# Context rows of a decoder block turned on the host instead of on TensorE

## What is computed

```python
q = query @ Wq + bq
kvp = kv @ Wkv + bkv            # kv: the context, (8, 750, 512)
k, v = jnp.split(kvp, 2, axis=-1)
...
scores = jnp.einsum('bhqd,bhkd->bhqk', q, k) * scale + bias[None]
attn = jax.nn.softmax(scores, axis=-1)
```

## Time and profile before

| | |
|---|---|
| median of 3 runs | 1767.23 us (1766.71 to 1767.92) |
| span of the profiled execution | 1770.0 us |
| TensorE matmul busy | 1686.0 us (95%) |
| TensorE weight load busy | 1356.3 us (77%) |
| VectorE busy | 1073.6 us (61%) |
| ScalarE busy | 746.3 us (42%) |
| GpSimd busy | 750.8 us (42%) |
| middle phase | about 164 to 697 us |

### The profile page before, as it was taken

How to read it: one execution, slowest core, us unless ns; L and a number is a source line. 1 busy time by engine, 2 the same in 40 slices (tenths; PEclk the granted TensorE clock), 3 DMA queues, 4 the chain that set the end, 5 groups by cost and what they waited for, 6 DMA issues and landing times. The chain is left out here.

```text
span 1770.0 us, 34943 instructions
## 1 busy us (share of the span) xinstructions
PE 1686.0 (95%) x11125; PEld 1356.3 (77%) x11125; DVE 1073.6 (61%) x1895; ACT 746.3 (42%) x1345; POOL 750.8 (42%) x852
## 2 busy tenths in 40 slices
PE   7999999999999998898998999899999999999998
PEld 6787778887887777676777677678888888888876
DVE  5554465555565555777888888764664546446653
ACT  3224333343344425665556464522442424224441
POOL 3100332323333325878878657541542424215441
PEclk9999999999999999999999999999999999999999
DMA  7736766666665857999787676345564737346773
GB/s 217 243 138 174 213 184 176 185 174 176 171 190 167 217 143 148 186 204 173 169 183 161 144 155 169 92 136 184 179 233 107 243 97 245 101 140 206 239 247 89
DMA packets 211842, 309.53 MB, mean 175 GB/s; under 512 B 21856, under 2 KB 151600, under 8 KB 207232
## 3 DMA queue, kind: packets, MB, share of 16 engines
q1 hardware_dynamic: 191584, 232.40, 50.0%
q0 software_dynamic: 15392, 41.02, 10.6%
q10 hardware_dynamic: 4752, 34.61, 5.2%
HBM read 224.30 MB, written 83.66 MB: 174 GB/s over the span
## 5 line engine op out<-in xcount | busy, mean ns | idle before, releaser
L2193 DVE TENSOR_REDUCE part_max<-a_s_bank 112x1 f32<-112x500 f32 (+1 forms) x368 | 224.3, 670 | 58.6 <-PE a_s_bank L1913 44.8
L2088 ACT ACTIVATE a_prob<-a_st_bank 125x448 f32<-125x448 f32 x384 | 196.4, 545 | 110.7 <-PE a_st_bank L1936 93.9
L2899 DVE TENSOR_TENSOR e_u_sb<-e_u_bank,e_b_row 128x512 f32<-128x512 f32 x134 | 92.3, 689 | 229.8 <-PE e_u_bank L2656 215.0
L2654 PE MATMUL e_u_bank<-e_w_hi,e_xT_hi 128*128 128x512 f32 x536 | 214.3, 400 | 0.9 <-DVE e_w_lo L2892 0.4
L2655 PE MATMUL e_u_bank<-e_w_lo,e_xT_hi 128*128 128x512 f32 x536 | 209.9, 392 | 0.0
L2656 PE MATMUL e_u_bank<-e_w_hi,e_xT_lo 128*128 128x512 f32 x536 | 209.5, 391 | 0.0
L2715 ACT ACTIVATE e_g_hi<-e_g_bank 128x256 fp32r<-128x256 f32 x133 | 51.0, 384 | 343.1 <-PE e_g_bank L2663 341.1
L2816 POOL DMA_INDIRECT out<-l_rows,e_y_row x33 | 52.9, 1604 | 290.0 <-DVE l_rows L2942 163.3
L1763 POOL TENSOR_TENSOR a_part_sum<-a_prob 125x448 f32<-125x448 f32 x128 | 148.4, 1164 | 25.3 <-ACT a_prob L2088 25.0
L997 POOL TENSOR_TENSOR m_prob_sum<-m_prob 112x224 f32<-112x224 f32 x128 | 85.3, 670 | 157.7 <-ACT m_prob L1249 150.6
L2792 POOL TENSOR_TENSOR e_w_lo<-e_w_raw,e_w_hi 128x1024 fp32r<-128x1024 f32 x28 | 102.7, 3678 | 48.9 <-ACT e_w_hi L2725 48.9
(11 more groups left out here) (428 smaller groups left out, 4368.7 us busy)
## 6 DMA issues: line engine op xcount, KB each, us to landing
e_w_raw<-L_ffn_Wl SPq DMA_DIRECT2D x96, 512.0 KB, 10.9
e_b_row<-L_ffn_bl ACTq DMA_DIRECT2D x33, 1024.0 KB
k<-m_kt_hi SPq DMA_DIRECT2D x48, 250.0 KB, 3.8
k<-m_kt_lo SPq DMA_DIRECT2D x48, 250.0 KB, 4.8
m_c_in<-ctx POOLq DMA_DIRECT2D x12, 896.0 KB, 6.8
v<-m_cv SPq DMA_DIRECT2D x48, 224.0 KB
a_v_sb<-v SPq DMA_DIRECT2D x32, 336.0 KB
m_q_st<-q SPq DMA_DIRECT2D x93, 112.0 KB, 3.1
```

Of the source, the lines that this page charges most:

```text
L2088: act.activation(prob[s % 2][:, hh, 2 * u:2 * u + 2, :], st_bank[n % SB][0:CR, 0:2 * S].rearrange("p (e q) -> p e q", e=2), ACT.Exp).then_ ...
L2193: dve.tensor_reduce(out, scores, AX.X, ALU.max).then_inc(s_free, 1)
L2654: pe.matmul(out, xT_hi[:, slot, k, :], w_h, start=(k == 0), stop=False)
L2899: dve.tensor_tensor(u_sb[:, q % 2, :, :], u_bank[q % 2][:, :].rearrange("p (h n) -> p h n", h=2), b1_row[:, slot, :, HC * q:HC * q + HC], ...
```

## The change

The host, which already orders the context rows, also lays them out turned: 12 chunks of [128 partitions, 4 blocks, 500 rows], so that `c_in` is [128, 4, 500] and one DMA fills it. `turn_ctx` is gone. ScalarE's copy and VectorE's subtraction read `c_in` in SBUF, at their old places in the order. ScalarE waits for the load, VectorE for ScalarE (`chi_ready`), TensorE's first key unit of a chunk for VectorE (`c_split`), and the next load for VectorE's last subtraction. The context leaves the shared sequence of turns.

```diff
-                whole = ctx[0:4 * CR, :].rearrange(rows_p, p=CR)
-                for a, z in row_parts(CR):
-                    pool.dma_start(c_in[a:z, :, :], whole[a:z, :, :]).then_inc(ctx_loaded, DMA)
+                pool.dma_start(c_in[:, :, :], ctx[0]).then_inc(ctx_loaded, DMA)
...
                         if ch + 1 < CHUNKS:
                             turn_h(ch + 1, t)
-                        else:
-                            turn_ctx(t)
...
+                def ctx_hi(kk):
+                    act.wait_ge(ctx_loaded, DMA)
+                    act.activation(first_ctx[0][:, kk, :], c_in[:, kk, :], ACT.Copy).then_inc(chi_ready, 1)
...
-                            turned(("h", CHUNKS, t), first_ctx[0][:, t, :], 4 * CR)
+                            ctx_hi(t)
...
+                def ctx_lo(kk):
+                    dve.wait_ge(chi_ready, kk + 1)
+                    dve.tensor_tensor(first_ctx[1][:, kk, :], c_in[:, kk, :], as_f32(first_ctx[0][:, kk, :]), ALU.subtract).then_inc(c_split, 1)
...
-                            turned_lo(("h", CHUNKS, t), first_ctx[1][:, t, :], first_ctx[0][:, t, :], 4 * CR)
+                            ctx_lo(t)
...
-                c, m = unit_of(unit_at(s, hh))
-                note(prod_at, "ctx", c, m)
-                if m >= KT and c + 1 < CHUNKS:
-                    note(turn_at, "ctx", c + 1, m - KT)
+                note(prod_at, "ctx", *unit_of(unit_at(s, hh)))
...
                 def load_ctx(ch):
                     if ch > 1:
-                        pool.wait_ge(t_ready, turn_at["ctx", ch - 1, KT - 1] + 1)
+                        pool.wait_ge(c_split, KT * (ch - 1))
                         pool.sem_inc(turn, 1)
-                    whole = ctx[CN * ch:CN * ch + CN, :].rearrange(rows2, p=CR)
-                    for a, z in row_parts(CR):
-                        pool.dma_start(c_in[a:z, :, :], whole[a:z, :, :]).then_inc(ctx_loaded, DMA)
+                    pool.dma_start(c_in[:, :, :], ctx[ch]).then_inc(ctx_loaded, DMA)
...
-                def turn_ctx(ch, kk):
-                    bank = bank_for_turn("ctx", ch, kk)
-                    if kk == 0:
-                        pe.wait_ge(ctx_loaded, ch * v_parts * DMA)
-                    for t in range(CT):
-                        last = pe.transpose(bank[:, CR * t:CR * t + CR], c_in[:, t, P * kk:P * kk + P], ident[0:CR, 0:CR])
-                    last.then_inc(t_ready, 1)
...
-                    splits = [split_at["ctx", ch, kk] + 1 for kk in range(KT)] if m == 0 and ch else None
+                    splits = (c_split, [KT * (ch - 1) + kk + 1 for kk in range(KT)]) if m == 0 and ch else None
...
-                        if ch + 1 < CHUNKS:
-                            turn_ctx(ch + 1, m - KT)
...
-                        turned(("ctx", ch + 1, m - KT), cT_hi[(ch + 1) % 2][:, m - KT, :], CN)
+                        act.wait_ge(ctx_loaded, (ch + 1) * DMA)
+                        act.activation(cT_hi[(ch + 1) % 2][:, m - KT, :], c_in[:, m - KT, :], ACT.Copy).then_inc(chi_ready, 1)
...
-                            turned_lo(("ctx", ch + 1, kk), cT_lo[j][:, kk, :], cT_hi[j][:, kk, :], CN)
+                            dve.wait_ge(chi_ready, ch * KT + kk + 1)
+                            dve.tensor_tensor(cT_lo[j][:, kk, :], c_in[:, kk, :], as_f32(cT_hi[j][:, kk, :]), ALU.subtract).then_inc(c_split, 1)
...
-                          kept("m_c_in", [CR, 4, D]), kept("m_b_col", [P, 2, KT]))
+                          kept("m_c_in", [P, KT, 4 * CR]), kept("m_b_col", [P, 2, KT]))
...
-    arrays["ctx_1024"] = np.ascontiguousarray(arrays["ctx_1024"][:, order, :])
+    rows = arrays["ctx_1024"][:, order, :].reshape(B * CTX // (4 * CR), 4 * CR, KT, P)
+    arrays["ctx_1024"] = np.ascontiguousarray(rows.transpose(0, 3, 2, 1))
```

More of the change, by code:

```diff
@@ L172, in opening_phase @@
             note(prod_at, "wv", ch, t)
-            note(turn_at, "h", ch + 1, t)
+            if ch + 1 < CHUNKS:
+                note(turn_at, "h", ch + 1, t)
             for hh in scores_at(ch, t):
@@ L215, in opening_phase @@
         ctx_loaded = c.sem("p_ctx_loaded")
+        chi_ready = c.sem("p_chi_ready")
+        c_split = c.sem("p_c_split")
         bias_loaded = c.sem("p_bias_loaded")
@@ L410, in turn_h @@
                     last.then_inc(t_ready, 1)
-                def turn_ctx(kk):
-                    bank = bank_for_turn("h", CHUNKS, kk)
-                    if kk == 0:
-                        pe.wait_ge(ctx_loaded, len(row_parts(CR)) * DMA)
-                    for t in range(4):
-                        last = pe.transpose(bank[:, CR * t:CR * t + CR], c_in[:, t, P * kk:P * kk + P], ident[0:CR, 0:CR])
-                    last.then_inc(t_ready, 1)
                 def project(n, ch, m):
@@ L823, in middle_phase @@
         ctx_loaded = c.sem("m_ctx_loaded")
+        chi_ready = c.sem("m_chi_ready")
+        c_split = c.sem("m_c_split")
         x_loaded = c.sem("m_x_loaded")
@@ L1038, in products @@
                         if splits:
-                            pe.wait_ge(t_split, splits[n])
+                            pe.wait_ge(splits[0], splits[1][n])
                         pe.matmul(out, a_hi, b_hi, start=(n == 0), stop=False)
@@ L1111, in project_q @@
                     for m in range(KT):
-                        splits = [split_at["h", b, kk] + 1 for kk in range(KT)] if m == 0 else None
+                        splits = (t_split, [split_at["h", b, kk] + 1 for kk in range(KT)]) if m == 0 else None
                         bank = bank_for_products("q", b, m)
@@ L3061, in build @@
     flat = "b s d -> (b s) d"
-    x, ctx = d["x"].rearrange(flat), d["ctx_1024"].rearrange(flat)
+    x, ctx = d["x"].rearrange(flat), d["ctx_1024"]
     q1, k1, q2 = (scratch(n, [GROUPS, 2, P, TOK]) for n in ("q1", "k1", "q2"))
```

## The result

The changed kernel took 1740.11 us in the median (1738.49 to 1742.89), beside 1766.97 for the kernel before (1764.82 to 1767.92): a ratio of 0.9858 [0.9843, 0.9873], which is 25.1 us; the two medians differ by 26.9. Forecast were 1745.1 us and a range of 1739 to 1752. The profiled execution of the changed kernel has a span of 1736.8 us, 33.2 less than that of before.

A forecast was written before the change was run, and what follows sets the result against it. TensorE was taken as the bound from 190 to 626 us. Savings of 13.3 + 4.8 + 2.7 + 1.3 = 22.1 us from the median of 1767.23 gave 1745.1 us, range 1739 to 1752.

The forecast's parts named there:

- the three signs: Wrong if the subtraction shows long outliers, TensorE waits for it at a chunk's first key product, or the 3.4 us transfer wait changes.
- Later slots: Second or third slots of a middle-phase step: 31 turn groups removed, each saving TensorE 0.43 us, 13.3 us in all.
- First slots: First slots of a step, 13 groups: ten gain 0.35 us, VectorE being late next, three gain 0.43; 4.8 us.
- The wait for the bank: Second hidden-row block no longer waits for a turn bank held by the context: 3 x 0.97 - 0.2 = 2.7 us.
- The opening: Opening phase: three of its four turn groups count at 0.43 us, 1.3 us; the fourth is hidden by a store.
- VectorE's subtraction at 0.67: Per context block, subtraction with both inputs in SBUF lasts 0.67 us, so VectorE's work does not change.
- Rival (a): VectorE's subtraction waits for a GpSimd sum of 0.67 us at 14 places, losing 9.4 us: 1754.5 us; chance 7%.
- The start of the middle: First chunk load beside loads TensorE awaits 3.4 us: taken as 0, bounds 6.4 us gained or as much lost.
- The later load: Next chunk's load starts about 1 us later, after VectorE's last subtraction; hidden, some 2 us left at worst landing.
- rival (d): Chunk load comes late, stalling ScalarE, VectorE and TensorE at 10 reloads; at 20.4 us landing, 1809 us; chance 3%.
- (b): Removed turns cost their full duration on TensorE, 192 x 0.268 = 51.5 us, giving 1715.7 us; chance 1%.
- (c): TensorE isn't the bound; another chain takes over everywhere, the 44 groups bring nothing: 1766 us; chance 3%.

The follow-up runs named there:

- idle_turns: Changed kernel with four idle TensorE turns put back ahead of each of 44 middle-phase value products, nobody waiting for them: 1759.38 us, beside 1743.04 for the changed kernel.
- one_sbuf_input: Changed kernel with VectorE's subtraction replaced by an equally long instruction reading one input from PSUM and one from SBUF, low part left out: 1741.49 us.
- early_lo: Changed kernel with VectorE's subtraction put ahead of the value rows' addition, in the middle and the opening: 1737.88 us, ratio 0.9838 to the kernel before.
- one_input: Changed kernel with VectorE's subtraction replaced by a multiplication of the landed block alone by 0, low part left out: 1742.02 us, ratio 0.9856.
- after: The changed kernel, run and profiled three times without further edits: 1740.11, 1743.04 and 1741.22 us; ratios to the kernel before 0.9858, 0.9876 and 0.9868.
- before_pieces: Kernel before with the chunk loaded in pieces of 8192 bytes instead of 2048, still as two DMAs, turns kept: 1764.21 us, ratio 0.9992.
- before again: The kernel before, unchanged, run once more for a second profile: 1770.1 us, one execution.

## Why the prediction was right

The time lies in the range, and the terms that carried it were measured one by one. But two of the three signs that the prediction named for being wrong did appear: the subtraction has long outliers, and the 3.4 us wait for a transfer has changed. They pull in opposite directions, 2.2 us against 2 to 3, and that they nearly cancel is luck.

- *Later slots, 31 x 0.43 = 13.3.* The slot went from 0.84 to 0.42; matched instructions move by 0.35 at the scores and by 0.08 at the next product, 0.43. Right, and `idle_turns` shows the same price when only the turns are put back.
- *First slots, 0.35 each.* 2.51 to 2.14 as read above, 0.37. Right, and so is the reason, that VectorE is late next: `one_sbuf_input` loses 0.23 us in these ten slots for 0.2 more on VectorE, `early_lo` and `one_input` gain 0.17 in them, and the three with hidden rows between change by at most 0.04.
- *The wait for the bank, 2.7.* -0.94 at each of four places, predicted 0.97; in the late step 0.97 comes back as part of the wait of 1.18 us. 4 x 0.94 - 0.97 = 2.8. Right.
- *The opening, 1.3.* 1.1 to 1.3 in three profiles. Right.
- *VectorE's subtraction at 0.67, at no cost.* Half right. The median is 0.67, but the sum lacked three collisions that cost TensorE 0.72 us each, 2.2 us in all. Rival (a) named the mechanism and was wrong in the partner, the places and the price: it took GpSimd's sums of 0.67 us at 14 places, 9.4 us; it was GpSimd's bias addition of 2.40 us at three. The step that failed is the look at GpSimd's queue. The case against (a) was argued from the order of the sums, and the bias additions were not looked up. The trace of before would also have shown that the two engines get in each other's way, in the scaling of x above, with a wait of TensorE behind it. The collisions with sums do happen, at no cost to TensorE that the traces show. By the rule of the Trainium skill cited there ("SBUF — State Buffer", "Who interferes with whom") this case had to come wherever the two overlap, and the trace agrees: 2.56 us beside GpSimd's 2.40. The same section ("SBUF — State Buffer", "Who interferes with whom") also has a one-input tensor-scalar in its faster mode among those that block, which agrees with the 0.41 us and the outliers of 2.4 us in `one_input`.
- *The stretch of the turns as a whole.* 13.3 + 4.8 + 2.7 = 20.8 predicted, 19.8 to 19.9 measured. The three collisions take 2.2, and the three waits behind the scaling of x give 1.0 back: 19.6. The prediction priced the GpSimd issue that goes at nothing, and that is where this 1.0 comes from.
- *The start of the middle, taken as 0.* This is the term that was mis-sized. "The bytes in flight stay the same" was true and didn't settle the wait. The three profiles of after are 2.7 to 3.9 us shorter there, and TensorE waits for a transfer 0.3 us in one of them and not in the others; those of before are at 0 and -1.5. At the same granted clock, 1.00, it is 3.9 against 1.5. The bounds of 6.4 either way covered it. How much of it is the change's isn't settled: `early_lo` and `one_sbuf_input`, with the same load at the same time, have waits of 3.7 and 2.5 us again and gain 0.5 and 0.0. That the wait comes from running beside the first chunk load is shown by the kernels with a later load: none of the four waits for those keys there, and all four are at -4.6 or -4.7. That the shorter hold on the DMA engines is what mostly takes it away in after is only argued, and `before_pieces` speaks against the pieces alone doing it.
- *The later load, hidden.* Landing took 9.5 us at most in after (11.9 in `early_lo`), and no TensorE wait for the context is among the waits of after. Right, and rival (d) did not come near. Rivals (b) and (c) fall by `idle_turns`.

The sum by what was measured: 19.9 in the turns, 1.2 in the opening, 2 to 3 at the start of the middle, 23 to 24 us in all, against 21.9, 23.3 and 25.1 by the ratios of three comparisons.

## What to carry to other kernels

Price a removed TensorE instruction by the distance from its start to the next start in two otherwise equal slots, and then ask which chain ends next behind it; that gave 0.43 us for four turns that each last 0.27. When an operand moves from PSUM to SBUF on VectorE, go through GpSimd's long instructions one by one, and not only its frequent ones, and put the new instruction where no due maximum stands behind it. When the shape of a transfer changes, don't take its bytes as the measure of what it does to others, and start it after the loads that somebody is already waiting for: one changed line took the wait away in every kernel that had it, and was worth 4.5 us by the medians here, 0.7 to 1.9 of them shown in the trace.

## What the runs showed of the hardware

- A VectorE subtraction of 0.67 us with two inputs in SBUF took 2.56 us beside a GpSimd addition of 2.40 us; started ahead of it, it made the addition last 2.91. With one of two inputs in PSUM no instance did, in 44. One input out of SBUF is no protection for a multiplication at 0.41 us for 500 columns (2.4 us, three times), nor for the scaling of x (0.89 instead of 0.53 to 0.58); batch statistics out of SBUF, at 0.68 to 0.70 us, were never longer beside a sum.
- A load of 1.02 MB held the DMA engines for 24.0 to 25.6% of 20 us as two transfers of 112 and 13 rows, whether in 160 or 288 packets, and for 15.8 to 19.8% as one of 128 rows.
- The same idle time can be followed by a fall of the granted clock or not. In both profiles of the kernel before TensorE sat idle for 1.60 us ahead of the same turn of the maxima. Behind it the mean clock over five microseconds was 0.66 in before again and 1.00 in the first profile (windows view, in this order):

```profile
590.00:595.00 5.00, 5.00 (x38) 3.58 (x37) 3.11 (x4) 1.45 (x2) 0.85 (x3) 0.66 0.94 240
```
```profile
592.00:597.00 5.00, 5.00 (x47) 3.80 (x45) 3.11 (x4) 1.45 (x2) 1.30 (x4) 1.00 0.93 240
```

This is 1.6 of the +1.8 us of before again in the stretch of the turns, nearly as much as the three collisions together. Single profiles of this kernel must be compared with such falls in mind.
